# A new front for a one-core Flamingo block: fillers, zeroing by transfers, compact values, paired tiles, another order

## The reference, cut to what matters

```python
x = x + tanh(g_xattn[0]) * L0_xattn(layernorm(x), ctx)
x = x + tanh(g_ffn[0])   * L0_ffn(layernorm(x))
x = x + tanh(g_xattn[1]) * L1_xattn(layernorm(x), ctx, ctx)
x = x + tanh(g_ffn[1])   * L1_ffn(layernorm(x))
```

## Time and profile before

| what | us |
| --- | --- |
| runs | 178.82, 179.99, 181.32 |
| median | 179.99 |
| the profiled execution, own time | 180.58 |
| its span in the trace | 178.8 |
| busy: PE / DVE / ACT / POOL | 157.2 / 107.2 / 85.8 / 64.0 |

### The profile page before, as it was taken

How to read it: one execution, slowest core, us unless ns; L and a number is a source line. 1 busy time by engine, 2 the same in 40 slices (tenths; PEclk the granted TensorE clock), 3 DMA queues, 4 the chain that set the end, 5 groups by cost and what they waited for, 6 DMA issues and landing times.

```text
span 178.8 us, 3338 instructions
## 1 busy us (share of the span) xinstructions
PE 157.2 (88%) x1254; PEld 106.5 (60%) x1254; DVE 107.2 (60%) x296; ACT 85.8 (48%) x146; POOL 64.0 (36%) x95
## 2 busy tenths in 40 slices
PE   0599997699999989999897999998986789999994
PEld 0256883574479984764443444444543676599994
DVE  1558757798543456799986889885332578302032
ACT  2124636262027205657975877878961047601120
POOL 6479914886374613089900000000020446000000
PEclk9999999569999999999999999999999969999999
DMA  5999910005588593001440000000004200000002
GB/s 154 392 333 425 402 53 2 0 2 139 132 169 172 108 335 126 4 11 33 72 64 2 0 0 0 4 0 4 0 0 128 110 2 2 0 4 0 4 0 66
DMA packets 4294, 15.43 MB, mean 86 GB/s; under 512 B 948, under 2 KB 1844, under 8 KB 3492
## 3 DMA queue, kind: packets, MB, share of 16 engines
q1 hardware_dynamic: 2980, 11.66, 21.1%
q10 hardware_dynamic: 576, 2.44, 3.9%
q0 software_dynamic: 720, 1.09, 2.9%
HBM read 13.94 MB, written 1.25 MB: 85 GB/s over the span
## 4 chain that ended last, share of the span: by engine, by line
PE 69%; POOL 9%; DVE 8%; DMA 5%; ACT 4%; issue 3%; POOLq 0%; ACTq 0%
PE bank L483 63%; PE bank L487 5%; DMA fc1T_sb<-q_rows 3%; POOL fc1T_sb L462 2%; POOL q_rows L457 2%; DVE stats L1178 2%; DMA x_sb<-in_x 2%; POOL rstd L372 1%; ACT arena L1136 1%; POOL xb L391 1%; DVE normed L1183 1%; DVE meanvar L1179 1%; DVE res_b L1234 1%; DVE mx L1373 1%; PE bank L907 1%
## 5 line engine op out<-in xcount | busy, mean ns | idle before, releaser
L1373 DVE TENSOR_REDUCE mx<-bank 128x1 f32<-128x512 f32 x64 | 42.0, 688 | 6.5 <-PE bank L483 6.1
L1100 ACT ACTIVATE arena<-bank 128x1024 f32<-128x1024 f32 x32 | 32.1, 1025 | 9.6 <-PE bank L483 9.0
L368 POOL TENSOR_SCALAR rstd<-meanvar 128x2 f32<-128x2 f32 x10 | 2.2, 225 | 62.2 <-DVE meanvar L1179 62.2
L483 PE MATMUL bank<-kpack,fc1T_sb 72*128 72x512 bf16 x64 | 22.7, 383 | 1.8 <-DMA fc1T_sb<-q_rows 1.1
L483 PE MATMUL bank<-fc1T_sb,kpack 104*128 104x256 bf16 x128 | 19.3, 272 | 0.1
L483 PE MATMUL bank<-arena,va 128*32 128x256 f32 x256 | 18.6, 387 | 0.5 <-ACT outT L1094 0.5
L483 PEld LDWEIGHTS bank<-fc1T_sb,kpack 104*128 104x128 bf16 x128 | 12.0, 97 | 6.2 <-issue 1.6
L483 PEld LDWEIGHTS bank<-kpack,fc1T_sb 72*128 72x128 bf16 x64 | 6.1, 97 | 12.3 <-issue 5.4
L487 PE MATMUL bank<-const_sb,normed 128*128 128x128 f32 x16 | 4.3, 338 | 8.6 <-DVE normed L1183 8.6
L483 PE MATMUL bank<-selq_bf,zeros_bf 128*128 128x512 bf16 (+1 forms) x49 | 11.4, 373 | 0.0
L483 PEld LDWEIGHTS bank<-arena,va 128*32 128x32 f32 x256 | 6.2, 108 | 6.8 <-issue 4.3
(11 more groups left out here) (232 smaller groups left out, 303.7 us busy)
## 6 DMA issues: line engine op xcount, KB each, us to landing
kpack<-k_parts SPq DMA_DIRECT2D x3, 768.0 KB
fc1T_sb<-in_fc1T SPq DMA_DIRECT2D x1, 2048.0 KB, 11.8
fc_sb<-in_fc SPq DMA_DIRECT2D x1, 2048.0 KB, 16.1
fc_sb<-in_gateup ACTq DMA_DIRECT2D x2, 1024.0 KB, 6.3
arena<-in_down SPq DMA_DIRECT2D x1, 1024.0 KB, 4.7
k_parts<-arena SPq DMA_DIRECT2D x8, 96.0 KB, 2.2
fc1T_sb<-q_rows POOLq DMA_DIRECT2D x9, 64.0 KB, 3.0
ctxT_sb<-in_ctxT SPq DMA_DIRECT2D x2, 256.0 KB, 4.7
```

Of the source, the lines that this page charges most:

```text
L368: pool.tensor_scalar(rstd[:, k, i:i + 2].unsqueeze(2), meanvar[:, k, i:i + 2, 1:2], EPS, None, ALU.add)\
L483: return pe.matmul(o, lhsT, rhs, start=start, stop=stop, **k)
L1100: act.activation(probs1[:, n % (2 * GH), :, :], bank[:, 2 + 2 * (n % 2):4 + 2 * (n % 2), :], ACT.Exp, scale=SCALE)\
L1373: dve.tensor_reduce(mx1[:, b * 2 + qt, g * GH + j:g * GH + j + 1], bank[:, r, :], AX_X, ALU.max)\
```

## The change

It rewrites what happens before the gate logits, and three things behind:

- `quiet`, a tile of 512 bf16 zeros, is set by VectorE first of all; TensorE runs 11 fillers on it before its first work. ScalarE runs a Tanh on a zero column at the start; the real Tanh comes behind the query copies.
- `w0` comes in two transfers, query and key weights first.
- Keys of batch 0 come ahead of the turned tiles. Tiles are turned, copied and multiplied to queries in pairs (256 columns). The order of VectorE is: tiles 0 and 1 normalised, bias columns, masked keys 0, tiles 2 and 3, masked keys 1; the mask column of `va0` is written behind tile 1 of the softmax.
- The bias product and its copy stand ahead of scores 3; values come in two batches. On TensorE each `weighted0(i)` follows directly on `probs0_turned(i)`, for i from 1. The residual of tile 0 comes before the division of tile 3.
- The zero rows of `kpack` and `qpack` are written by transfers from `quiet`, issued by SP: `kpack` behind all loads, `qpack` once the experts' first product is done.
- `va1` has 9 columns a head instead of 32 (8 values and the one), and only the ones are set by GpSimd. `weighted` writes 9 of each 32 rows.

```diff
+        quiet = sb("quiet", [P, T], BF16)
+        zeros_bf = quiet[:, 0:P]
...
-        va1 = sb("va1", [P, NB * KC, H, 32])
+        va1_flat = sb("va1_flat", [P, 3328])[:]
+        va1 = va1_flat[:, 0:NB * KC * H * (DH + 1)].rearrange("p (c h w) -> p c h w", c=NB * KC, h=H)
...
-            sp.wait_ge(S["kpack_zero"], 1)
+            sp.wait_ge(S["quiet_set"], 1)
+            sp.dma_start(kpack[NROW:KROWS, :, :].rearrange("p h s -> p (h s)").rearrange("p (n t) -> p n t", t=T),
+                         quiet[NROW:KROWS, :].unsqueeze(1).to_broadcast([KROWS - NROW, H * NB * SK // T, T]))\
+                .then_inc(S["kpack_zero"], 16)
+            sp.wait_ge(S["kpack_zero"], 16)
...
+            sp.wait_ge(S["fc1_ps"], PR0)
+            sp.dma_start(qpack[NROW:MROW, :, :, :].rearrange("p b h t -> p (b h t)").rearrange("p (n t) -> p n t", t=T),
+                         quiet[NROW:MROW, :].unsqueeze(1).to_broadcast([MROW - NROW, NB * H * SQ // T, T]))\
+                .then_inc(S["qpack_zero"], 16)
             sp.wait_ge(S["pv1_ps"], UNITS)
...
-            pool.memset(va1[:], 0.0).then_inc(S["va1_zero"], 1)
-            pool.wait_ge(S["va1_zero"], 1)
-            pool.memset(va1[:, :, :, DH:DH + 1], 1.0).then_inc(S["va1_zero"], 1)
-            pool.wait_ge(S["va1_zero"], 2)
-            pool.memset(late[ZROW:P, :], 0.0).then_inc(S["kpack_zero"], 1)
-            pool.wait_ge(S["kpack_zero"], 1)
+            pool.memset(va1[:, :, :, DH:DH + 1], 1.0).then_inc(S["va1_ones"], 1)
...
-            pool.memset(fc1T_sb[ZROW:MROW, :, :], 0.0).then_inc(S["qpack_zero"], 1)
-            pool.wait_ge(S["qpack_zero"], 1)
...
+            pe.wait_ge(S["quiet_set"], 1)
+            for _ in range(11):
+                mm(bank[:, 7, 0:T], zeros_bf, quiet[:])
+            pe.wait_ge(L["w0"], 16)
+            pe.wait_ge(L["ctx"], 16)
+            keys0(0)
+            pe.wait_ge(L["const"], 16)
+            normed0_turned(0)
+            normed0_turned(1)
+            pe.wait_ge(L["ctx_b"], 16)
+            keys0(1)
+            queries0(0)
+            normed0_turned(2)
+            normed0_turned(3)
+            scores0(0)
+            scores0(1)
+            queries0(1)
+            scores0(2)
+            pe.wait_ge(S["bvcol_set"], 2)
+            pe.wait_ge(L["w0_b"], 16)
...
+            mm(bank[:, 0, 0:D], bvcol[:, 0, :], w0_sb[:, 3, :], stop=False)
...
+            values0(0)
+            scores0(3)
             probs0_turned(0)
+            values0(1)
+            weighted0(0)
             probs0_turned(1)
-            weighted0(0)
+            weighted0(1)
             probs0_turned(2)
-            weighted0(1)
+            attention0_turned(0)
+            weighted0(2)
             probs0_turned(3)
-            weighted0(2)
-            attention0_turned(0)
             attention0_turned(1)
+            project0(0)
             weighted0(3)
-            project0(0)
+            project0(1)
             attention0_turned(2)
-            project0(1)
+            project0(2)
             attention0_turned(3)
-            project0(2)
             project0(3)
...
+                if n == 0:
+                    pe.wait_ge(S["qpack_zero"], 16)
...
-                    ins = mm(bank[32 * j:32 * j + 32, 6, 0:SQ], va1[:, b * KC + kc, g * GH + j, :],
+                    ins = mm(bank[32 * j:32 * j + DH + 1, 6, 0:SQ], va1[:, b * KC + kc, g * GH + j, :],
...
-            act.dma_start(w0_sb[:], w0).then_inc(L["w0"], 16)
-            act.wait_ge(L["gates"], 16)
-            act.activation(tanhg[:], gates_sb[:], ACT.Tanh).then_inc(S["tanh_done"], 1)
+            act.dma_start(w0_sb[:, 0:2, :], w0[:, 0:2, :]).then_inc(L["w0"], 16)
+            act.dma_start(w0_sb[:, 2:4, :], w0[:, 2:4, :]).then_inc(L["w0_b"], 16)
+            act.wait_ge(S["quiet_set"], 1)
+            act.activation(tanhg[:, 0:1], quiet[:, 0:1], ACT.Tanh)
...
+            probabilities(0)
+            probabilities(1)
+            act.wait_ge(S["bias_ps"], 1)
+            act.copy(bias[:, 0, :], bank[:, 0, 0:D]).then_inc(S["bias_sb"], 1)
+            probabilities(2)
+            probs0_copied(0)
+            probs0_copied(1)
+            probabilities(3)
+            probs0_copied(2)
+            attention0_copied(0)
+            probs0_copied(3)
+            for i in range(1, NT):
+                attention0_copied(i)
...
+            dve.memset(quiet[:], 0.0).then_inc(S["quiet_set"], 1)
             dve.wait_ge(L["x"], 16)
...
+            for i in range(3):
+                attention0(i)
+            residual0(0)
+            attention0(3)
+            for i in (1, 2, 3):
+                residual0(i)
```

More of the change, by code:

```diff
@@ L510, in scores0, with values0 @@
                 mm(bank[:, 4 + i, :], q0T[:, i, :], k0[:, i // 2, :]).then_inc(S["sc0_ps"], 1)
[L512 to L538, removed]
+            def values0(b):
+                for c in range(b * KC, (b + 1) * KC):
+                    mm(bank[:, 2 + b, (c % KC) * P:(c % KC + 1) * P], ctxT_sb[:, c * P:(c + 1) * P],
+                       w0_sb[:, 2, :]).then_inc(S["v0_ps"], 1)
             def probs0_turned(i):
@@ L1005, in _ @@
             act.wait_ge(L["small"], 16)
-            copies("nT0_ps", "nT0_sb", lambda i: normedT[0][:, i, :], lambda i: bank[:, 4 + i, 0:P])
-            for i in range(NT):
-                act.wait_ge(S["q0_ps"], i + 1)
-                act.activation(q0T[:, i, :], bank[:, 2 + i % 2, 0:P], ACT.Identity, bias=vec(V_BQ)).then_inc(S["q0_sb"], 1)
-            for i in range(NT):
+            for half in range(2):
+                act.wait_ge(S["nT0_ps"], 2 * half + 2)
+                act.copy(normedT[0][:, 2 * half:2 * half + 2, :].rearrange("p i t -> p (i t)"), bank[:, 4 + 2 * half, 0:SQ])\
+                    .then_inc(S["nT0_sb"], 2)
+                act.wait_ge(S["q0_ps"], 2 * half + 2)
+                act.activation(q0T[:, 2 * half:2 * half + 2, :].rearrange("p i t -> p (i t)"), bank[:, 2 + half, 0:SQ],
+                               ACT.Identity, bias=vec(V_BQ)).then_inc(S["q0_sb"], 2)
@@ L1011, in _, with probabilities @@
+            act.wait_ge(L["gates"], 16)
+            act.activation(tanhg[:], gates_sb[:], ACT.Tanh).then_inc(S["tanh_done"], 1)
+            def probabilities(i):
                 act.wait_ge(S["shift0"], i + 1)
                 act.activation(probs0[:, i, :], shifted[:, i, :], ACT.Exp, scale=SCALE).then_inc(S["probs0_sb"], 1)
-                if i == 0:
-                    act.wait_ge(S["bias0_ps"], 1)
-                    act.copy(bias[:, 0, :], bank[:, 0, 0:D]).then_inc(S["bias0_sb"], 1)
-                else:
-                    act.wait_ge(S["p0T_ps"], i)
-                    act.copy(probs0T[:, i - 1, :], bank[:, i - 1, :]).then_inc(S["p0T_sb"], 1)
@@ L1019, in _, with probs0_copied, attention0_copied @@
[L1019 to L1021 removed]
+            def probs0_copied(i):
+                act.wait_ge(S["p0T_ps"], i + 1)
+                act.copy(probs0T[:, i, :], bank[:, i, :]).then_inc(S["p0T_sb"], 1)
+            def attention0_copied(i):
+                act.wait_ge(S["attT0_ps"], i + 1)
+                act.copy(attT[0][:, i, :], bank[:, i, 0:P]).then_inc(S["attT0_sb"], 1)
@@ L1046, in _ @@
                          .rearrange("p (h d) -> p h d", d=DH)).then_inc(S["va1_sb"], 1)
-            act.wait_ge(S["bias1_ps"], 1)
-            act.copy(bias[:, 1, :], bank[:, 6, 0:D]).then_inc(S["bias1_sb"], 1)
+            act.wait_ge(S["bias_ps"], 2)
+            act.copy(bias[:, 1, :], bank[:, 6, 0:D]).then_inc(S["bias_sb"], 1)
             act.wait_ge(S["yn_sb"], NT)
@@ L1188, in _, with masked_keys @@
                 ln_stats(0, i, x_sb[:, i, :])
-            for i in range(NT):
-                ln_apply(0, i)
-            dve.wait_ge(L["const"], 16)
             he = const_sb[:, K_HE:K_HE + H]
             hs = const_sb[:, K_HS:K_HS + H]
-            dve.tensor_copy(va0[:, :, :, DH:DH + 1],
-                            hs.unsqueeze(1).unsqueeze(3).to_broadcast([P, NB * KC, H, 1]))
-            dve.wait_ge(L["small"], 16)
-            for b in range(NB):
+            def masked_keys(b):
                 dve.wait_ge(S["k0_ps"], b + 1)
@@ L1203, in _ @@
                     .then_inc(S["k0_sb"], 1)
+            for i in (0, 1):
+                ln_apply(0, i)
+            dve.wait_ge(L["small"], 16)
             for l, v in ((0, V_BV), (1, V_BV1)):
                 dve.tensor_copy(bvcol[:, l, :], vec(v).to_broadcast([P, P])).then_inc(S["bvcol_set"], 1)
+            dve.wait_ge(L["const"], 16)
+            masked_keys(0)
+            for i in (2, 3):
+                ln_apply(0, i)
+            masked_keys(1)
             def masked_v(b):
@@ L1222, in _, with attention0 @@
                     .then_inc(S["shift0"], 1)
+                if i == 1:
+                    dve.tensor_copy(va0[:, :, :, DH:DH + 1],
+                                    hs.unsqueeze(1).unsqueeze(3).to_broadcast([P, NB * KC, H, 1]))
                 if i >= 2:
                     masked_v(i - 2)
```

(4 more changed lines are left out.)

62 lines of the change are left out of this document (27 added, 35 removed).

## The result

The changed kernel is slower: 182.53 us (four runs, 181.07 to 183.5) against 180.34 us for the kernel before, measured beside it; ratio 1.0134, interval 1.0074 to 1.0193. The forecast was 178.2 us with a range from 175.8 to 180.6. The profiled execution took 182.66 us with a span of 180.8 us against 178.8, and its last statement on VectorE starts 1.95 us later than before. So the miss to be explained, in the profiles, is 1.95 us lost where 1.8 us were to be gained, 3.75 us in all.

A forecast was written before the change was run, and what follows sets the result against it. It took TensorE to bound the second attention and the softmax from 18.6 us, after a slow-clocked start. 180.58 - 1.35 (front) - 0.45 (compact values) = 178.8 us profiled, 178.2 us against the median; range 175.8 to 180.6 us.

The forecast's parts named there:

- Fillers and table: At the start: 11 fillers from about 1.2 to 6.0 us, clock rising near 6.4 us, delaying nothing over 0.3 us.
- First scores: Start of layer 0's softmax: the first maximum moves from 13.37 to 10.3 us, 3.1 us gained.
- Weighting 0: Layer 0's softmax on TensorE: the first weighting starts at 16.85 us instead of 19.9, still 3.1 us ahead.
- What gives it back: Layer 0's softmax: exposed ScalarE copies make a tile 2.1 us instead of 1.42; three steps cost 2.05, leaving 1.05 us.
- Tail: From the last attention tile to the gate logits: their maximum at 32.37 us comes 1.35 us earlier.
- Middle: From the scores on: nothing reordered, fillers and grade shift alike; taken as 0, bounds -0.75 and +1.3 us.
- Zeroing by transfers: Zero rows of key and query packs by transfer instead of GpSimd memsets: covered, cost 0.
- Compact values: Weightings of layer 1 load 9 columns instead of 32: 0.45 us gained, bounds 0 and 2.6 us.
- A: Rival: the whole front's gain arrives, 3.1 us or more; 176.4 us, 175.7 with the middle; chance 0.17.
- B: Rival: loading the values' weights spaces layer 1's weightings, 2.6 us gained instead of 0.45; 176.1 us; chance 0.08.
- C: Rival: TensorE's clock rises late or falls back in the new softmax's gaps; 183.4 us; chance 0.10.
- D: Rival: compact rows no longer run four abreast in layer 1's weightings, 38 us lost; 217 us; chance 0.02.

The follow-up runs named there:

- e1: The changed kernel with each tile's transposes set back ahead of the weighting of the tile before; 179.92 us, ratio 1.0012 to the kernel before.
- e3: The changed kernel with the edits of e1 and e2 together; 177.84 us, ratio 0.9888 to the kernel before.
- e8: e3 with the key pack's zero rows written by GpSimd again instead of by the 1 MB transfer; 177.83 us, ratio 0.9912.
- e13: e3 with the weights of layer 0 in one transfer instead of two; 178.51 us.
- e4: The kernel before, with the gate logits' maximum taken four times in a row instead of once; 181.83 us, ratio 1.012.
- e2: The changed kernel with GpSimd's first subtraction of the key parts made to wait for VectorE's score product; 179.99 us, ratio 1.0025 to the kernel before.
- e10: e4 with GpSimd's subtraction made to wait for the score product, as in e2; 180.8 us, ratio 1.0032 to the kernel before.
- e9: e7 with 28 fillers again instead of 24 ahead of the grade; 178.01 us, ratio 0.984 to the kernel before.
- e5: The kernel before with only the compact values, 9 columns a head in layer 1 instead of 32; ratio 0.9989.
- e7: e3 with ScalarE copying turned tiles and taking the logits' exponential before casting layer 1 keys, and 24 fillers instead of 28 ahead of the grade; 177.83 us, ratio 0.9818.
- e12: e8 unchanged, run again for a second look at the context's landing; 177.43 us.

## Why the prediction was wrong, point by point

- *Fillers and table.* Right in what they do. Fillers from 1.18 us (forecast 1.2); their last ends near 5.1 us instead of 6.0, since the clock rose near 4.0 us and not near 6.4. That was this execution: in the profiles of the experiments the same 11 fillers take between 3.9 and 4.9 us (4.87 in e1 and e3), so the rise came up to about 2 us later in others, and the forecast's 4.8 us lies at the end of that. The first keys wait for their weights until 5.50 us, 0.5 us before the forecast.
- *First scores.* Forecast 10.3 us, measured 10.83. The step that failed is the landing of the second half of the context, taken as 4.9 us after issue from the earlier trace rows, measured 5.8. Where it landed 5.0 to 5.2 us after issue (e3, e8, e13), the first maximum came at 10.44 to 10.46 us; so the landing is about 0.4 us of the 0.53. Splitting the weights, which I had costed at nothing, is the likely cause. TensorE's order left VectorE never late there, as forecast.
- *Weighting 0.* Forecast 16.85 us, measured 17.64: the 0.53 us of before, and 0.26 us more in the steps between.
- *What gives it back.* The mechanism was right (each copy exposed), the term mis-sized: 2.36 us a tile instead of 2.1. I had added the copy to 1.42 us, which is the distance of overlapping rows. Once the copy waits for the transposes, and those stand behind the weighting, the ends count as well: 1.25 + 0.45 + 0.59 and 0.07 us of handing over. Three steps: 7.03 us measured (17.64 to 24.67) against 6.3, 0.73 us. e1 gives the whole back: last weighting at 22.45 us.
- *Tail.* The chain named (keys of layer 1, ScalarE, logits) was the right one: VectorE waits 0.51 us for the logits, and no more for its own statistics. The last weighting began 0.79 + 0.73 = 1.52 us late; 0.34 us more were lost behind it, since it takes 1.25 us where I had 1.0 and the last projections now wait one by one for their copies. So the maximum came at 32.88 us where I had 32.37 - 1.35 = 31.02, 0.51 us after the old one. That is 1.86 of the 3.75 us.
- *Middle.* "From the scores on nothing is reordered", taken as 0: this term, put at nothing, is the step that failed worst. The order on each engine was the same, but the offset between VectorE and GpSimd was not. The score product came 0.25 us after GpSimd's subtraction instead of 0.37 us before it and took 1.91 us instead of 0.19: 1.72 us, 46% of the miss. I had the like before me in the bias columns (0.83 to 0.89 us each beside GpSimd's zeroing, 0.36 for both without it), and did not look for it here. VectorE is released when the subtraction ends, in the changed kernel, e1 and e4 alike (0.04, 0.04 and 0.05 us behind its end); what the two engines share there, no run shows. e2 and e10 show that nothing else is behind it: the order of the two alone changes the product's length. The 2.6 us behind the +1.3 of the range were my estimate, from no row; the stretch at 0.50 ahead of the grade lasted 6.8 us in both kernels and 3.4 us in e2 and e9.
- *Zeroing by transfers.* Right in cost (0; for the key pack e8 shows it by undoing it). The 1 MB landed 22.6 us after issue, at about 29.9 us, between the 25.6 and 33 us that the forecast's two rates gave, and the ones rows were issued at 29.85. The key parts followed at 39.36, no later than before.
- *Compact values.* 0.3 us instead of 0.45. Forty nanoseconds a group speak against weight loading as what spaces the products; what does space them was not tried. Where the forecast has 213 and 53 ns, the kernel before shows 216 and 54: single records of 256 fp32 columns start 216 ns apart (138.8 to 140.7 us), and at their closest so do every four records of the weightings in layer 1.
- *Rivals.* A, the whole front, did not come even with the order kept: e3 gained 2.0 us (177.84 beside a before of 179.87) of the 3.5 that A had down, and A's 176.4 us lies below e3's interval, which on 179.99 us reaches down to 176.8. B falls with e5. C, the clock falling in the gaps of the new softmax, did not happen: granted 1.00 from 17.6 to 26 us, the products there kept the faster speed (1.25 us a weighting, as for the first one in the kernel before, in the row below). D did not happen. The case that came, an expected gain small enough for one collision to turn its sign, stood in none of the rivals, and my range had left 0.6 us above the median of before for it. One sum of the chances was wrong: slower than 183.6 us was put at 0.05, where half of C and D make 0.07, so that 0.80 and not 0.82 was left for the rest.

```profile
19.95 1.25 PE L483 MATMUL bank<-va,arena 128*128 128x144 f32 x8 [0.24 <-ACT arena L1018]
```

The terms close: 1.86 (front) + 1.72 (collision) + 0.15 (compact values) = 3.73 of the 3.75 us. That they close so well is in part luck, since it is one profile of each kernel and executions of one kernel differ by 1.4 us or more. On the way the two do differ: the grade is 2.43 us late where front and collision give 2.26, and 0.48 us come back behind it, of which the compact values explain 0.3.

## What to carry to other kernels

When a front is made faster or slower, list the instructions of VectorE and GpSimd that stood close to each other in time, with their distance, and not only the ones in the path: a margin of 0.37 us between two engines was worth 1.7 us here, and one wait on a semaphore (e2) made that pair safe. It does so for one pair only: the next subtraction of GpSimd still cost VectorE 0.84 us in e7. Where a copy by another engine stands between two products of TensorE, put the next tile's transposes ahead of this tile's weighting; and cost a step whose overlap is lost from the full lengths of its rows, not from their distance.

## What the runs showed of the hardware beyond that

The gain of e9 over e3 went missing in the tail, and the clock is the likely reason; it was read from traces and not tried. From the end of the second attention on, TensorE waits much (2.43 of 4 us busy in 134 to 138 us in the kernel before), and the granted clock falls once for some microseconds (in every profile but that of e12; to 0.50 at 144.7 to 148.1 us in the kernel before, at 134.8 to 138.1 us in e13). Where it falls and rises differs from execution to execution. In e3 it lay at 134 to 142 us (granted 0.74 and 0.83 in its two halves), and 142 to 150 us ran at 1.00. The busy time by windows, columns as in the earlier trace rows, in e8 and in e9, whose groups of four heads begin together (95.57 and 95.58 us):

```profile
142.00:146.00 4.00, 4.00 (x20) 3.00 (x17) 3.66 (x16) 2.36 (x5) 3.02 (x5) 0.71 0.01 2
146.00:150.00 4.00, 4.00 (x34) 2.25 (x33) 3.36 (x12) 2.79 (x6) 1.83 (x2) 1.00 0.02 4
```

```profile
142.00:146.00 4.00, 4.00 (x15) 3.18 (x13) 3.66 (x16) 1.96 (x5) 3.04 (x5) 0.50 0.01 2
146.00:150.00 4.00, 4.00 (x24) 1.99 (x23) 2.12 (x5) 2.10 (x4) 1.75 (x2) 0.77 0.00 0
```

The same 26 records of the shared expert, from the chains of waits:

```profile
141.69 5.19 PE bank L482 x26
```

```profile
141.61 6.97 PE bank L482 x26
```

5.19 us (5.39 in the kernel before) against 6.97 us: 1.8 us from the place of one dip, and the spans differ by 1.7 us (175.2 and 176.9). Where a kernel was timed four times or more, its executions spread by 1.4 to 3.8 us; this dip, and the one before the grade, are large enough to make most of such a spread, though that was not tested by itself. So whether a front that is 1 us faster is worth 1 us at the end can't be told from one profile.
